# Inverting the softmax sums inside the attention stages, and splitting later weights on GpSimd in the first one

## The chip, the cores and the metric

The kernel runs on one core of a Trainium2 chip. The metric is the device time of one execution in microseconds (us), as the median of several runs. The program is one chain of stages on one core: every engine takes part in every stage, and a barrier of all engines stands between two stages.

## The reference

Two cross-attention layers run one after the other. x is 4096 x 512, the context 3202 x 512, all in float32. The first layer has 8 heads of 16, the second 16 heads of 32.

```
q, k, v  = projections of x (or of its layernorm) and of the context
attn     = softmax(q k^T / sqrt(hd));   o = attn v
layer 1:   X = x + o W_o;      x1  = relu(X w1^T + b1) w2^T + b2 + X
layer 2:   q from layernorm(x1);  X = x1 + o Wo^T + bo;  out = X + silu(X W1^T + b1) W2^T + b2
```

The attention kernels store the unnormalised `exp(...) v` (`acc`) and the row sums (`sums`); the stage behind divides. Products of float32 matrices are built from three TensorE products of halves: a matrix is split into `hi` (rounded to the TensorE's float32r) and `lo` (what is left), and `hi hi + hi lo + lo hi` is accumulated.

## The kernel before

The stages are `front` (keys, values, first queries), `attention` "a0" (layer 1), `middle` "m" (the rest of layer 1, layernorm, second queries), `attention` "a1" (layer 2) and `ending` "e".

**Attention.** An *item* is one head and one block of 512 queries: 64 items in a0, 128 in a1. A head's keys fill 26 tiles of 128. For an item TensorE computes 26 score tiles (L535), ScalarE the exponentials (L441), TensorE the weighted sums of v in batches (L561). For the items ahead, TensorE computes scores a second time in 28 *units* (L526) and VectorE reduces each from PSUM (L465), which gives the row maximum; SP moves it through DRAM into the query tile (`move_row`, L336 and L340). In a0 the sums of the exponentials come from a column of ones in v. In a1 GpSimd adds up most exponential tiles in nine steps per item (L407 to L421), VectorE adds six others (L482), and a last matmul with ones (L556) finishes the sum. ScalarE copies the accumulator out (L428), SP stores it (L346 to L353).

SP issues all transfers of a stage in the order of its program: per item the query tile of the next item (`a_q`, L331), the query tile of the maxima of the item after that (`a_qm`, L331), the store of the item before, `move_row`, and at each head's first item the keys and values of the head after it (`load_kv`, L320 and L324). TensorE's first unit that reads a newly loaded `a_qm` stands at tile 14 of the 26 of an item.

**Weights.** In a0 VectorE splits Wo of layer 2 in the last item (`split_weights`, L488 and L490), and SP stores the halves to DRAM. In a1 the four row blocks of W1 are loaded whole at the start (L362) and split by VectorE in the last item ahead of its work of that item; the halves stay in SBUF for the ending. The middle stage loads W_o, w1, w2 and splits them itself on ScalarE and VectorE (L1647, L1724).

**Start of the middle and of the ending.** SP loads all sums as 128 rows (`total`), VectorE inverts them (L1802, L1448), SP stores them to DRAM (`recips`) and loads them back, each head's row spread over the partitions of that head (L1597, L1297). Only then can the first block be normalised (L1731, L1415) and split, which TensorE's first product (L1857, L1484) waits for. In the middle TensorE then computes the query bias (L1907) from Wq, which is the last transfer that SP issues there, and only after it the first hidden layer.

Of the kernel before, what the change touches and what calls it, by code (L numbers as in the profile page):

```python
# [26 lines left out]
P = 128  # L27
# [157 lines left out]
def attention(nc, name, H, hd, q, k, v, row, acc_out, sums_out, weights=(), keep=()):  # L185
# [17 lines left out]
    with phase(nc, name) as (ctx, sb, ps, sem):  # L203
# [5 lines left out]
        prob = sb("prob", [P, ST, NB], F32)  # L209
        acc_sb = [sb(f"acc_sb{i}", [P, NB], F32) for i in range(2)]  # L210
# [21 lines left out]
        ones_made = sem("ones_made")  # L232
        add_done, acc_copied, vsum_done = sem("add_done"), sem("acc_copied"), sem("vsum_done")
# [3 lines left out]

        w_loaded, w_hi, w_lo, w_kept = sem("w_loaded"), sem("w_hi"), sem("w_lo"), sem("w_kept")

# [5 lines left out]
        SPLIT_AT = 0  # L245
# [59 lines left out]

        q_items = q.rearrange("h b s r c -> (h b) s r c")
# [3 lines left out]
        def _(sp):  # L310
# [30 lines left out]

            def store(h, qb, j, n):
                sp.wait_ge(acc_copied, n + 1)
                cols = bass.ds(qb * NB, NB)
                for i in range(ATEND):
                    sp.dma_start(acc_out[i, bass.ds(h * hd, hd), cols],  # L346
                                 acc_sb[j][i * 32:i * 32 + hd, :]).then_inc(acc_stored[j], 16)
                if APART:
                    sp.wait_ge(side_copied, n + 1)
                    sp.dma_start(acc_out[ATEND, bass.ds(h * hd, hd), cols], side[3 * 32:P, :]).then_inc(side_stored, 16)  # L350
                for i in range(SUMS):
                    at = 3 * 32 if APART else i * 32 + hd
                    sp.dma_start(sums_out[i, bass.ds(h, 1), cols],  # L353
                                 acc_sb[j][at:at + 1, :]).then_inc(acc_stored[j], 16)
# [38 lines left out]
            sp.wait_ge(w_kept, 16 * len(keep))  # L393

        @block.gpsimd
        def _(pool):
            fill(pool, 1)

# [61 lines left out]
        def _(dve):  # L460
# [24 lines left out]
            def split_weights():  # L485
                dve.wait_ge(w_loaded, 16 * len(weights))
                for i, (_, whole, hi, lo) in enumerate(weights):
                    dve.tensor_copy(hi, whole).then_inc(w_hi, 1)  # L488
                    dve.wait_ge(w_hi, i + 1)
                    dve.tensor_tensor(lo, whole, f32(hi), ALU.subtract).then_inc(w_lo, 1)  # L490
# [11 lines left out]
            for it in items(dve):  # L502
                for t in range(ST):
                    if it.last and weights and t == SPLIT_AT:

                        split_weights()
# [7 lines left out]
            if weights:  # L514
                dve.wait_ge(w_lo, len(weights))
# [702 lines left out]
def ending(nc, name, acc, sums, recips, x, wo_split, bo, W1, b1, func, w2, b2, out):  # L1218
# [22 lines left out]
    spread = [t.rearrange("h (c t) -> (h c) t", c=P // H) for t in (sums[0], recips)]  # L1241

    with phase(nc, name) as (ctx, sb, ps, sem):
# [8 lines left out]

        total = h[1]
        assert H * T // P == NB
# [32 lines left out]
        def _(sp):  # L1287
# [12 lines left out]
            def next_acc(n, k):  # L1300

                sp.wait_ge(ol_done, n * KT + k)
                load_acc(n, k)
                load_recips(n, k)
# [28 lines left out]
            load_wo(0, 3)  # L1333
            for m in range(FT):
# [72 lines left out]
        def _(dve):  # L1407
# [39 lines left out]
            dve.wait_ge(sums_loaded, 16)  # L1447
            dve.reciprocal(total[:], total[:]).then_inc(recip_done, 1)  # L1448
            for k in range(KT):
                normalise(0, k)  # L1450
                split_o(0, k)
            for d in range(KT):
                add_x(0, d)
# [70 lines left out]
def middle(nc, name, acc, sums, recips, x, wo, w1, b1, w2, b2, gamma, beta, wq, x1, q):  # L1524
# [13 lines left out]
    spread = [t.rearrange("h (c t) -> (h c) t", c=P // H) for t in [sums[i] for i in range(SIDE)] + [recips]]  # L1538

    with phase(nc, name) as (ctx, sb, ps, sem):  # L1540
# [5 lines left out]
        total = sb("total", [P, SIDE, H * T // P], F32)  # L1546
# [18 lines left out]
        staged = {"wo": (std[:].unsqueeze(1), WO), "w1": (y[:], W1), "w2": (early[0], W2)}  # L1565
# [20 lines left out]
        W_ORDER = ["wo", "w1", "w2", "wq"]  # L1586
# [3 lines left out]
        def _(sp):  # L1590
# [14 lines left out]

            for i in range(SIDE):
                sp.dma_start(total[:, i], spread[i]).then_inc(sums_loaded, 16)
            load_weight("wo", staged["wo"][0], wo)
            load_acc(0)
            load_weight("w1", staged["w1"][0], w1)  # L1610
            for to, dram in ((bias1[:], b1), (bias2[:], b2), (gb[:, 0, :], gamma), (gb[:, 1, :], beta)):
                sp.dma_start(to, dram[:, :]).then_inc(const_loaded, 16)
            sp.wait_ge(recip_done, 1)
            sp.dma_start(spread[SIDE], total[:, 0]).then_inc(recips_stored, 16)
            load_xin(0)
            sp.wait_ge(recips_stored, 16)
            load_recips(0)
            load_weight("w2", staged["w2"][0], w2)
            load_weight("wq", sq[:], wq)
            for n in range(-1, BLOCKS + 1):  # L1620
                if 0 <= n + 2 < BLOCKS:

                    sp.wait_ge(ol_done, n + 2)
                    load_acc(n + 2)
                    load_recips(n + 2)
# [17 lines left out]
        def _(act):  # L1643
            def split_weight(n):
                stage, (hi, _) = staged[n]
                act.wait_ge(w_loaded[n], 16)
                act.activation(hi[:], stage, ACT.Copy).then_inc(w_hi, 1)  # L1647

# [40 lines left out]
            split_weight("wo")  # L1689
            split_weight("w1")  # L1690
            split_o(0)
            split_weight("w2")
# [7 lines left out]
            act.wait_ge(w_lo, len(W_ORDER))  # L1700
# [19 lines left out]
        def _(dve):  # L1720
            def split_weight(i, n):
                stage, (hi, lo) = staged[n]
                dve.wait_ge(w_hi, i + 1)
                dve.tensor_tensor(lo[:], stage, f32(hi[:]), ALU.subtract).then_inc(w_lo, 1)  # L1724

# [71 lines left out]
            dve.memset(inv_d[:], 1.0 / D).then_inc(consts_done, 1)  # L1797
            dve.wait_ge(sums_loaded, 16 * SIDE)
# [4 lines left out]
            split_weight(0, "wo")  # L1803
            split_weight(1, "w1")
            normalise(0)
            split_o(0)
            split_weight(2, "w2")
            add_x(0)
            split_x(0)
# [4 lines left out]
            dve.wait_ge(w_hi, 4)  # L1814
# [36 lines left out]
        def _(pe):  # L1851
# [16 lines left out]
            def hidden(n):  # L1868
                pe.wait_ge(xl_done, n + 1)
                if n == 0:  # L1870
                    pe.wait_ge(w_lo, 2)
# [5 lines left out]
            def project(n, tiles):  # L1877
                if n == 0:
                    pe.wait_ge(w_lo, 3)
# [7 lines left out]
            def queries(n):  # L1887
                pe.wait_ge(ycl_done, n + 1)
                if n == 0:
                    pe.wait_ge(w_lo, 4)  # L1890
# [10 lines left out]
            pe.wait_ge(w_lo, 1)  # L1901
# [35 lines left out]
def build(nc, a, out):  # L1937
# [20 lines left out]
    wo_split = scratch("wo_split", [KT, 2, P, KT, P])  # L1958
    with ExitStack() as ctx:
        WO = weight(nc, ctx, "wo", KT, D)  # L1960
        whole = ctx.enter_context(nc.sbuf_tensor("wo_whole", [P, KT, D], F32))
        attention(nc, "a0", *L0, q[0], k[0], v[0], row, acc[0], sums[0],
                  [(a["L1_xattn_Wo"].rearrange("(k p) c -> p k c", p=P), whole[:], WO[0][:], WO[1][:])],
                  [(wo_split[d, i], WO[i][:, :, d * P:(d + 1) * P]) for d in range(KT) for i in range(2)])
    middle(nc, "m", acc[0], sums[0], recips[0], x, a["L0_xattn_W_o"], a["L0_xattn_w1"], a["L0_xattn_b1"],
           a["L0_xattn_w2"], a["L0_xattn_b2"], a["L1_xattn_ln_q_g"], a["L1_xattn_ln_q_b"], a["L1_xattn_Wq"], x1, q[1])
    with ExitStack() as outer:
        W1 = weight(nc, outer, "w1", KT, a["L1_xattn_W1"].shape[1])
        with ExitStack() as inner:
            whole = inner.enter_context(nc.sbuf_tensor("w1_whole", [P, KT, a["L1_xattn_W1"].shape[1]], F32))  # L1970
            attention(nc, "a1", *L1, q[1], k[1], v[1], row, acc[1], sums[1],
                      [(src, whole[:, i, :], W1[0][:, i, :], W1[1][:, i, :])
                       for i, src in enumerate(rows(a["L1_xattn_W1"], a["L1_xattn_W1"].shape[1]))])
# [30 lines left out]
```

## Time and profile before

| what | value |
| --- | --- |
| median of 3 runs | 5425.91 us (5416.05 to 5426.97) |
| the profiled execution, its own time | 5431.3 us |
| its span | 5429.5 us |
| PE busy | 5216.4 us (96%) |
| VectorE (DVE) busy | 4277.0 us (79%) |
| ScalarE (ACT) busy | 3251.5 us (60%) |
| GpSimd (POOL) busy | 2485.7 us (46%) |
| DMA | 341.18 MB, 63 GB/s over the span |

The stages can be told apart by the tile names (`kv_`, `a_`, `m_`, `e_`). a0 and a1 both use `a_`; a0 ends and the middle begins at 1444 us, the middle's products end at 1819 us, a1 lasts until 4557 us, and the ending fills the rest. "SPq" rows are DMA issues of SP. The granted clock of TensorE (PEclk) is given as a share: 1.00 is 2.4 GHz, 0.50 is 1.2 GHz.

### The profile page before, as it was taken

How to read it: one execution, taken by the hardware profiler on the slowest of the kernel's cores; microseconds unless marked ns; L12 is line 12 of the kernel's file. 1: busy time of each engine (PE TensorE's matmuls, PEld its weight loads, DVE VectorE, ACT ScalarE, POOL GpSimd, SP SyncE). 2: the span in 40 equal slices, each digit the busy share in tenths (PEclk: the TensorE clock that was granted, in tenths of full speed). 3: DMA queues.
4: the chain of work that ended last, by engine and by line, in shares of the span. 5: the costliest groups of instructions: out<-in, count | busy, mean ns of one | idle time of the engine just before them, and what ended most of it. 6: DMA issues, size and time to landing. Idle time of an engine off the chain costs nothing. (4 is left out here: it accounts for less than half of the span.)

```text
span 5429.5 us, 93007 instructions
## 1 busy us (share of the span) xinstructions
PE 5216.4 (96%) x27916; PEld 3335.3 (61%) x27916; DVE 4277.0 (79%) x6970; ACT 3251.5 (60%) x5920; POOL 2485.7 (46%) x1165
## 2 busy tenths in 40 slices
PE   8989999999799799999999999999999995999999
PEld 6844444444377566666666666666666662788887
DVE  6689999999577799999999999999999995432331
ACT  4258888888533377777777777777777773322222
POOL 0000000000000299999999999999999995000000
PEclk9989999999799799999999999999999997999999
DMA  7521111111344311111111111111111112332320
GB/s 218 130 51 36 38 39 39 38 37 32 93 124 128 107 33 45 46 45 46 37 41 45 46 45 45 32 46 45 46 45 33 45 33 86 117 97 87 100 93 24
DMA packets 340342, 341.18 MB, mean 63 GB/s; under 512 B 188304, under 2 KB 196368, under 8 KB 337936
## 3 DMA queue, kind: packets, MB, share of 16 engines
q1 hardware_dynamic: 339984, 336.71, 23.5%
q8 instruction: 188, 3.08, 0.2%
q14 instruction: 170, 1.39, 0.1%
HBM read 227.57 MB, written 108.92 MB: 62 GB/s over the span
## 5 line engine op out<-in xcount | busy, mean ns | idle before, releaser
L465 DVE TENSOR_REDUCE a_maxes<-a_mscore 128x1 f32<-128x458 f32 (+4 forms) x5376 | 3044.8, 626 | 218.6 <-PE a_mscore L526 163.1
L441 ACT ACTIVATE a_prob<-a_score 128x512 f32<-128x512 f32 x4992 | 2635.6, 602 | 891.8 <-PE a_score L535 855.9
L535 PE MATMUL a_score<-a_q,a_k 97*128 97x512 f32 (+1 forms) x4992 | 1937.1, 434 | 23.6 <-ACT a_prob L441 8.0
L526 PE MATMUL a_mscore<-a_k,a_qm 96*128 96x458 f32 (+4 forms) x5376 | 1837.8, 412 | 36.1 <-DMA a_k<-k 33.9
L410 POOL TENSOR_TENSOR a_added<-a_added,a_prob 128x1024 f32<-128x1024 f32 x640 | 1533.7, 2396 | 71.0
L526 PEld LDWEIGHTS a_mscore<-a_k,a_qm 96*128 96x128 f32 (+1 forms) x5376 | 1456.4, 309 | 131.2 <-DVE a_maxes L465 49.8
L535 PEld LDWEIGHTS a_score<-a_q,a_k 97*128 97x128 f32 (+1 forms) x4992 | 916.1, 193 | 974.4 <-ACT a_prob L441 587.1
L561 PE MATMUL a_acc<-a_prob,a_v 128*32 128x512 f32 x9984 | 1469.1, 604 | 1.1 <-ACT a_prob L441 0.7
L304 POOL MEMSET a_k<- 32x126 f32 (+4 forms) x6 | 6.3, 1053 | 1821.9 <-POOLq L60 1821.6
L556 PE MATMUL a_acc<-a_prob,a_ones 128*1 128x512 f32 x1280 | 611.6, 592 | 0.0
L482 DVE TENSOR_REDUCE a_vsum<-a_prob 128x256 f32<-128x768 f32 x512 | 528.5, 1033 | 31.6 <-POOL a_added L416 30.3
L1438 DVE TENSOR_TENSOR e_hl<-e_h,e_hh 128x512 fp32r<-128x512 f32 x128 | 88.6, 692 | 533.0 <-ACT e_hh L1387 533.0
L561 PEld LDWEIGHTS a_acc<-a_prob,a_v 128*32 128x32 f32 x9984 | 276.6, 109 | 322.5 <-issue 205.9
L1383 ACT ACTIVATE e_h<-e_hp,e_bias 128x512 f32<-128x512 f32 x128 | 88.3, 690 | 562.5 <-PE e_hp L1495 562.5
L407 POOL TENSOR_TENSOR a_added<-a_prob 128x1024 f32<-128x1024 f32 x128 | 305.9, 2389 | 134.6 <-ACT a_prob L441 134.4
L416 POOL TENSOR_TENSOR a_added<-a_added,a_vsum 128x1024 f32<-128x1024 f32 x128 | 305.6, 2387 | 14.5 <-POOL a_added L413 0.4
L428 ACT ACTIVATE a_acc_sb<-a_acc 97x512 f32<-97x512 f32 (+1 forms) x192 | 114.7, 598 | 181.8 <-PE a_acc L556 176.2
L1495 PE MATMUL e_hp<-e_xh,w_hi 128*128 128x512 f32 x512 | 204.0, 398 | 7.6 <-DVE e_xl L1430 7.6
L1495 PE MATMUL e_hp<-e_xl,w_hi 128*128 128x512 f32 x512 | 203.0, 397 | 0.0
L1495 PE MATMUL e_hp<-e_xh,w_lo 128*128 128x512 f32 x512 | 203.0, 397 | 0.0
L413 POOL TENSOR_TENSOR a_added<-a_added,a_prob 128x512 f32<-128x512 f32 x128 | 166.9, 1304 | 14.5 <-ACT a_prob L441 0.4
L421 POOL TENSOR_TENSOR a_total<-a_added 128x512 f32<-128x512 f32 x128 | 166.1, 1298 | 10.0
(208 smaller groups left out, 4063.3 us busy)
## 6 DMA issues: line engine op xcount, KB each, us to landing
e_part<-acc SPq DMA_DIRECT2D x120, 256.0 KB, 3.8
a_qm<-q SPq DMA_DIRECT2D x384, 64.0 KB, 1.9
a_q<-q SPq DMA_DIRECT2D x384, 64.0 KB, 1.9
acc<-a_acc_sb SPq DMA_DIRECT2D x384, 64.0 KB
a_k<-k SPq DMA_DIRECT2D x48, 416.0 KB, 6.6
q<-m_qout SPq DMA_DIRECT2D x128, 128.0 KB, 2.3
e_wo<-wo_split SPq DMA_DIRECT2D x32, 512.0 KB, 4.9
k<-kv_k1out SPq DMA_DIRECT2D x24, 512.0 KB, 2.9
```

Of the source, the lines that this page charges most:

```text
L407: pool.tensor_tensor(added[:], prob[:, 0:2], prob[:, 10:12], ALU.add).then_inc(add_done, 1)
L410: pool.tensor_tensor(added[:], added[:], prob[:, t:t + 2], ALU.add).then_inc(add_done, 1)
L413: pool.tensor_tensor(added[:, 0], added[:, 0], prob[:, 22], ALU.add).then_inc(add_done, 1)
L416: pool.tensor_tensor(added[:], added[:], vsum[:], ALU.add).then_inc(add_done, 1)
L441: act.activation(prob[:, t], score[SCORES[it.j][t]][:], ACT.Exp, scale=SCALE).then_inc(exp_done, 1)
L465: dve.tensor_reduce(maxes[j][:, t, c:c + 1], mscore[u % UNIT_BANKS][:, 0:wide], AX.X, ALU.max).then_inc(unit_read, 1)
L482: dve.tensor_reduce(vsum[:, which, cols], prob[:, tiles[0]:tiles[-1] + 1, cols].rearrange("p t c -> p c t"), AX.X, ALU.add).then_inc(vsum_ ...
L526: pe.matmul(mscore[u % UNIT_BANKS][:, 0:wide], qm[j][r:r + ROW, t:NB:NB // P], kt[kk][r:r + ROW, at:at + wide], start=True, stop=True).the ...
L535: pe.matmul(score[SCORES[it.j][t]][:], kt[it.k][r:r + C, i * P:(i + 1) * P], qt[it.j][r:r + C, :], start=True, stop=True).then_inc(score_d ...
L556: mm = pe.matmul(acc[c * 32:c * 32 + 1, :], ones[:, col:col + 1], total[:] if what[0] == "sum" else prob[:, what[1]], start=start, stop=stop)
L561: mm = pe.matmul(acc[c * 32:c * 32 + 32, :], vt[kk][:, L.FIRST[half] + at, :], prob[:, what], start=start, stop=stop)
L1495: mm = pe.matmul(hp[m % 2][:], W1[a][:, k, m * P:(m + 1) * P], (xh, xl)[c][:, k], start=(t == 0), stop=(t == 3 * KT - 1))
```

## The change

Both attentions, in the last item, load the sums of all items but the last, add them up and invert them on VectorE, and store the reciprocals. The middle and the ending begin with `acc` and these reciprocals; they load the last item's sums as 128 x 4 numbers, invert those, and store them before the last block.

In a0 GpSimd splits W_o, w1, w2 of layer 1, Wo and the four row blocks of W1 of layer 2: eight jobs through one whole tile and two half tiles. SP runs them from `later_weights`, at each head's first item (ahead of `load_kv`) and at its sixth: it stores the halves of one job to DRAM and loads the next weight. The middle loads halves instead of whole weights; a1 loads the halves of W1, one of the eight at each such step. VectorE's `split_weights` goes.

```diff
 attention, SP:
-            for dram, whole, _, _ in weights:
-                sp.dma_start(whole, dram).then_inc(w_loaded, 16)
+            def later_weights(step):
+                if 0 <= step - 2 < len(splits):
+                    job = splits[step - 2]
+                    sp.wait_ge(w_lo, step - 1)
+                    for i, half in enumerate(halves):
+                        for c, to in enumerate(job[3]):
+                            wide = job[2] // len(job[3])
+                            sp.dma_start(to[i], f32(piece(half, job)[:, :, c * wide:(c + 1) * wide])).then_inc(w_kept, 16)
+                if 0 <= step - 1 < len(splits):
+                    job = splits[step - 1]
+                    if step > 1:
+                        sp.wait_ge(w_lo, step - 1)
+                    sp.dma_start(piece(whole, job), job[0]).then_inc(w_loaded, 16)
+                if 0 <= step - 1 < len(loads):
+                    to, dram = loads[step - 1]
+                    sp.dma_start(f32(to), dram).then_inc(w_loaded, 16)
...
+                if it.starts_head or (isinstance(it.qb, int) and it.qb == QB - 3):
+                    later_weights(it.h * 2 + (0 if it.starts_head else 1))
                 if it.starts_head and not it.first and not it.final_head:
                     load_kv(it.h + 1, 1 - it.k)
                 if it.last:
-                    for to, half in keep:
-                        sp.wait_ge(w_lo, len(weights))
-                        sp.dma_start(to, f32(half)).then_inc(w_kept, 16)
+                    sp.wait_ge(acc_stored[1 - it.j], H * (QB // 2) * STORED)
+                    sp.wait_ge(acc_stored[it.j], (H * (QB // 2) - 1) * STORED)
+                    for i in range(SUMS):
+                        sp.dma_start(sums_all[0:BUT_LAST, i], spread[i][0:BUT_LAST]).then_inc(sums_loaded, 16)
+                    sp.wait_ge(recip_done, 1)
+                    sp.dma_start(spread[SUMS][0:BUT_LAST], sums_all[0:BUT_LAST, 0]).then_inc(recips_stored, 16)
                     store(it.h, it.qb, it.j, it.n)
 attention, GpSimd:
+            for i, job in enumerate(splits):
+                pool.wait_ge(w_loaded, 16 * i + 16)
+                if i:
+                    pool.wait_ge(w_kept, KEPT[i])
+                hi, lo = (piece(half, job) for half in halves)
+                pool.tensor_copy(hi, piece(whole, job)).then_inc(w_hi, 1)
+                pool.wait_ge(w_hi, i + 1)
+                pool.tensor_tensor(lo, piece(whole, job), f32(hi), ALU.subtract).then_inc(w_lo, 1)
 attention, VectorE (split_weights goes; at tile 20 of the last item):
+            def invert():
+                dve.wait_ge(sums_loaded, 16 * SUMS)
+                for i in range(1, SUMS):
+                    dve.tensor_tensor(sums_all[0:BUT_LAST, 0], sums_all[0:BUT_LAST, 0], sums_all[0:BUT_LAST, i],
+                                      ALU.add).then_inc(summed, 1)
+                    dve.wait_ge(summed, i)
+                dve.reciprocal(sums_all[0:BUT_LAST, 0], sums_all[0:BUT_LAST, 0]).then_inc(recip_done, 1)
 ending, SP (VectorE inverts the last item's total behind the four first splits):
-            sp.dma_start(total[:], spread[0]).then_inc(sums_loaded, 16)
             load_acc(0, 0)
+            load_recips(0, 0)
             load_acc(0, 1)
+            load_recips(0, 1)
             for to, dram in ((biaso[:], bo), (bias1[:], b1), (bias2[:], b2)):
...
-            sp.wait_ge(recip_done, 1)
-            sp.dma_start(spread[1], total[:]).then_inc(recips_stored, 16)
-            sp.wait_ge(recips_stored, 16)
-            load_recips(0, 0)
-            load_recips(0, 1)
+            sp.dma_start(total[:], spread[0]).then_inc(sums_loaded, 16)
 middle, SP (split_weight goes on ScalarE and VectorE):
+            load_acc(0)
+            load_recips(0)
+            load_halves("wo", WO)
+            load_xin(0)
+            load_halves("w1", W1)
+            for to, dram in ((bias1[:], b1), (bias2[:], b2), (gb[:, 0, :], gamma), (gb[:, 1, :], beta)):
+                sp.dma_start(to, dram[:, :]).then_inc(const_loaded, 16)
+            load_halves("w2", W2)
             for i in range(SIDE):
                 sp.dma_start(total[:, i], spread[i]).then_inc(sums_loaded, 16)
...
             load_weight("wq", sq[:], wq)
```

## Rows read from the trace of the kernel before

**Rows 1.** Windows of a0 and a1: stretch, length, each engine's busy time, PEclk, DMA, GB/s

```profile
500.00:1380.00 880.00, 873.35 (x5352) 433.43 (x5348) 807.26 (x1467) 715.37 (x1364) 0.00 (x0) 1.00 0.17 37
2000.00:4490.00 2490.00, 2478.28 (x14065) 1545.54 (x14065) 2343.42 (x3933) 1770.02 (x3338) 2297.87 (x1073) 1.00 0.17 42
```

**Rows 2.** Timeline of POOL near a1's end: start, length, line, out<-in, count, idle before

```profile
4459.68 2.39 POOL L407 TENSOR_TENSOR a_added<-a_prob 128x1024 f32<-128x1024 f32 x1 [1.03 <-ACT a_prob L441]
...
4478.32 1.28 POOL L421 TENSOR_TENSOR a_total<-a_added 128x512 f32<-128x512 f32 x1
...
4501.28 2.38 POOL L407 TENSOR_TENSOR a_added<-a_prob 128x1024 f32<-128x1024 f32 x1 [0.47 <-ACT a_prob L441]
...
4526.36 3.19 POOL L421 TENSOR_TENSOR a_total<-a_added 128x512 f32<-128x512 f32 x1
...
4551.24 1.26 POOL L421 TENSOR_TENSOR a_total<-a_added 128x512 f32<-128x512 f32 x1
```

**Rows 3.** Line 490, VectorE's subtractions: ns min/median/max, first and last start

```profile
L490 DVE TENSOR_TENSOR w_lo<-w_whole,w_hi x4: 4309/4336/4357, 4509.8 to 4530.7; 128x2048 fp32r<-128x2048 f32 x4
```

**Rows 4.** Timeline of ACT near a1's end

```profile
4531.51 0.60 ACT L428 ACTIVATE a_acc_sb<-a_acc 97x512 f32<-97x512 f32 x1 [8.43 <-PE a_acc L556]
```

**Rows 5.** Timelines of SP, DVE and PE at the start of the ending

```profile
4559.27 0.36 SPq L1315 DMA_DIRECT2D e_h<-sums  x1
...
4569.88 3.35 DVE L1448 RECIPROCAL e_h<-e_h 128x512 f32<-128x512 f32 x1 [31.08 <-DMA e_bias<-in_L_xattn_b]
4579.29 2.14 DVE L1413 TENSOR_TENSOR e_part<-e_part 128x512 f32<-128x512 f32 x3 [6.06 <-DMA e_part<-recips]
...
4600.02 0.79 PE L1484 MATMUL e_ap<-e_oh,e_wo 128*128 128x512 f32 x1 [45.60 <-DVE e_ol L1419]
```

**Rows 6.** Timelines of SP, DVE and PE at the start of the middle

```profile
1444.19 1.78 SPq L1607 DMA_DIRECT2D m_total<-sums  x4
...
1456.59 3.57 SPq L1597 DMA_DIRECT2D m_part<-recips  x8
...
1461.76 2.15 DVE L1729 TENSOR_TENSOR m_part<-m_part 128x512 f32<-128x512 f32 x3 [1.80 <-DMA m_part<-recips]
...
1471.41 3.73 PE L1907 MATMUL m_var<-m_gb,m_sq 128*128 128x1 f32 x32
1475.55 0.77 PE L1857 MATMUL m_prod<-m_xh,m_w_hi 128*128 128x512 f32 x1 [0.41 <-issue]
```

**Rows 7.** Windows with busy DMA: the last two numbers are DMA share and GB/s

```profile
465.40:473.40 8.00, 7.93 (x46) 4.59 (x47) 7.60 (x15) 6.07 (x12) 0.00 (x0) 1.00 0.94 122
1846.00:1854.00 8.00, 8.00 (x16) 4.54 (x15) 7.96 (x16) 0.00 (x0) 0.00 (x0) 0.50 1.01 422
5336.00:5337.00 1.00, 1.00 (x7) 0.79 (x6) 0.69 (x1) 0.23 (x1) 0.00 (x0) 1.00 1.07 418
1446.00:1458.00 12.00, 0.00 (x0) 0.00 (x0) 3.90 (x6) 2.54 (x2) 0.00 (x0) 0.50 0.98 327
```

**Rows 8.** Timeline of SP in a0 at the first item of head 2

```profile
591.49 2.63 SPq L331 DMA_DIRECT2D a_q<-q  x6
...
604.28 2.62 SPq L320 DMA_DIRECT2D a_k<-k  x6
...
609.06 3.75 SPq L331 DMA_DIRECT2D a_q<-q  x6
613.01 2.67 SPq L331 DMA_DIRECT2D a_qm<-q  x6
```

**Rows 9.** Waits of PE in a0: waited for, us in total, times, longest

```profile
PE a_mscore L526 <- DMA a_qm<-q: 0.2, 1, 0.2
```

**Rows 10.** Timelines of SP and PE at a1's start

```profile
1852.68 0.33 SPq L336 DMA_DIRECT2D row<-a_negmax  x1
1856.38 0.24 SPq L340 DMA_DIRECT2D a_q<-row  x1
...
1857.95 0.76 PE L535 MATMUL a_score<-a_q,a_k 97*128 97x512 f32 x1 [1.23 <-DMA a_q<-row]
```

More of the change, by code:

```diff
@@ L182, with attention @@
 VSUMS = len(ON_VECTOR) * PIECES
-def attention(nc, name, H, hd, q, k, v, row, acc_out, sums_out, weights=(), keep=()):
+def attention(nc, name, H, hd, q, k, v, row, acc_out, sums_out, recips, splits=(), loads=()):
     SCALE = float(hd) ** -0.5
@@ L232, in attention @@
         ones_made = sem("ones_made")
+        sums_loaded, summed, recip_done, recips_stored = (
+            sem("sums_loaded"), sem("summed"), sem("recip_done"), sem("recips_stored"))
         add_done, acc_copied, vsum_done = sem("add_done"), sem("acc_copied"), sem("vsum_done")
@@ L235, in attention, with piece @@
         acc_stored = [sem(f"acc_stored{i}") for i in range(2)]
+        if splits:
+            whole = sb("whole", [P, KT * D], F32)
+            halves = [sb(f"half{i}", [P, KT * D], F32R) for i in range(2)]
         w_loaded, w_hi, w_lo, w_kept = sem("w_loaded"), sem("w_hi"), sem("w_lo"), sem("w_kept")
+        KEPT = [16 * sum(2 * len(job[3]) for job in splits[:i]) for i in range(len(splits) + 1)]
+        def piece(tile, job):
+            return tile[:, 0:job[1] * job[2]].rearrange("p (k c) -> p k c", k=job[1])
         LOADS = 16 * 3 * HALVES
@@ L243, in attention @@
         STORED = 16 * (ATEND + SUMS)
-        SPLIT_AT = 0
+        RECIP_AT = 20
         def items(eng):
@@ L304, in fill @@
                 eng.memset(ap, value).then_inc(filled[i], 1)
+        spread = [t.rearrange("h (c t) -> (h c) t", c=P // H) for t in [sums_out[i] for i in range(SUMS)] + [recips]]
+        BUT_LAST = P - P // (H * QB)
         q_items = q.rearrange("h b s r c -> (h b) s r c")
@@ L392, in _ @@
                 sp.wait_ge(side_stored, 16 * H * QB)
-            sp.wait_ge(w_kept, 16 * len(keep))
+            sp.wait_ge(w_kept, KEPT[-1])
+            sp.wait_ge(w_loaded, 16 * (len(splits) + len(loads)))
+            sp.wait_ge(recips_stored, 16)
         @block.gpsimd
@@ L483, in add_up @@
                                   AX.X, ALU.add).then_inc(vsum_done, 1)
[L485 to L490, printed above, removed]
+            def invert():
[5 more added lines that the diff above has]
+                dve.reciprocal(sums_all[0:BUT_LAST, 0], sums_all[0:BUT_LAST, 0]).then_inc(recip_done, 1)
             fill(dve, 0)
@@ L503, in _ @@
                 for t in range(ST):
-                    if it.last and weights and t == SPLIT_AT:
-                        split_weights()
                     for ahead, u in units_of(it, t):
@@ L513, in _ @@
                         add_up(it.n, it.first, *divmod(L.sum_at.index(t), PIECES))
-            if weights:
-                dve.wait_ge(w_lo, len(weights))
+                    if it.last and t == RECIP_AT:
+                        invert()
         @block.tensor
@@ L1239, in ending @@
     A_AT, ADD_AT = (11, 12, 13, 14), (12, 13, 14, 15)
-    spread = [t.rearrange("h (c t) -> (h c) t", c=P // H) for t in (sums[0], recips)]
+    spread = [t[H - 1, T - NB:T].rearrange("(p t) -> p t", p=P) for t in (sums[0], recips)]
     with phase(nc, name) as (ctx, sb, ps, sem):
@@ L1300, in next_acc @@
             def next_acc(n, k):
+                if n == BLOCKS - 1 and k == 0:
+                    sp.wait_ge(recips_stored, 16)
                 sp.wait_ge(ol_done, n * KT + k)
@@ L1333, in _ @@
             load_wo(0, 3)
+            sp.wait_ge(recip_done, 1)
+            sp.dma_start(spread[1], total[:]).then_inc(recips_stored, 16)
             for m in range(FT):
@@ L1451, in _ @@
                 split_o(0, k)
+            dve.wait_ge(sums_loaded, 16)
+            dve.reciprocal(total[:], total[:]).then_inc(recip_done, 1)
             for d in range(KT):
@@ L1521, in _, with middle @@
                 use_hidden(n, FT - 1)
-def middle(nc, name, acc, sums, recips, x, wo, w1, b1, w2, b2, gamma, beta, wq, x1, q):
+def middle(nc, name, acc, sums, recips, x, split, b1, b2, gamma, beta, wq, x1, q):
     H, BLOCKS, HT = sums.shape[1], T // NB, KT
@@ L1536, in middle @@
     HEADS = P // QD
-    spread = [t.rearrange("h (c t) -> (h c) t", c=P // H) for t in [sums[i] for i in range(SIDE)] + [recips]]
+    spread = [t[H - 1, T - NB:T].rearrange("(p t) -> p t", p=P) for t in [sums[i] for i in range(SIDE)] + [recips]]
     with phase(nc, name) as (ctx, sb, ps, sem):
@@ L1604, in load_weight, with load_halves @@
                 sp.dma_start(to, dram.rearrange("(k p) c -> p k c", p=P)).then_inc(w_loaded[n], 16)
+            def load_halves(n, to):
+                for half, dram in zip(to, split[n]):
+                    sp.dma_start(f32(half[:]), dram).then_inc(w_loaded[n], 16)
+            load_acc(0)
[6 more added lines that the diff above has]
+            load_halves("w2", W2)
             for i in range(SIDE):
                 sp.dma_start(total[:, i], spread[i]).then_inc(sums_loaded, 16)
[L1608 to L1618, printed above, removed]
             load_weight("wq", sq[:], wq)
@@ L1624, in _ @@
                     load_acc(n + 2)
+                    if n + 2 == BLOCKS - 1:
+                        sp.wait_ge(recip_done, 1)
+                        sp.dma_start(spread[SIDE], total[:, 0]).then_inc(recips_stored, 16)
+                        sp.wait_ge(recips_stored, 16)
                     load_recips(n + 2)
@@ L1720, in _ @@
         def _(dve):
[L1721 to L1724, printed above, removed]
             def normalise(n):
@@ L1797, in _ @@
             dve.memset(inv_d[:], 1.0 / D).then_inc(consts_done, 1)
+            normalise(0)
+            split_o(0)
+            add_x(0)
+            split_x(0)
             dve.wait_ge(sums_loaded, 16 * SIDE)
@@ L1958, in build @@
     wo_split = scratch("wo_split", [KT, 2, P, KT, P])
-    with ExitStack() as ctx:
[L1960 to L1973, printed above, removed]
+    F = a["L1_xattn_W1"].shape[1]
@@ new lines, in build, with tiles @@
+    first = {n: scratch(f"first_{n}", [2, P, kt, D]) for n, kt in (("wo", 1), ("w1", KT), ("w2", KT))}
+    w1_split = scratch("w1_later", [KT, 2, P, 1, F])
+    def tiles(w):
+        return w.rearrange("(k p) c -> p k c", p=P)
+    splits = [(tiles(a[f"L0_xattn_{n}"]), kt, D, [[first[m][i] for i in range(2)]])
+              for n, m, kt in (("W_o", "wo", 1), ("w1", "w1", KT), ("w2", "w2", KT))]
+    splits.append((tiles(a["L1_xattn_Wo"]), KT, D, [[wo_split[d, i] for i in range(2)] for d in range(KT)]))
@@ new lines, in build @@
+    splits += [(tiles(a["L1_xattn_W1"][r * P:(r + 1) * P, :]), 1, F, [[w1_split[r, i] for i in range(2)]])
+               for r in range(KT)]
+    attention(nc, "a0", *L0, q[0], k[0], v[0], row, acc[0], sums[0], recips[0], splits)
+    middle(nc, "m", acc[0], sums[0], recips[0], x, first, a["L0_xattn_b1"], a["L0_xattn_b2"], a["L1_xattn_ln_q_g"],
+           a["L1_xattn_ln_q_b"], a["L1_xattn_Wq"], x1, q[1])
+    with ExitStack() as ctx:
+        W1 = weight(nc, ctx, "w1", KT, F)
+        attention(nc, "a1", *L1, q[1], k[1], v[1], row, acc[1], sums[1], recips[1],
+                  loads=[(W1[i][:, r:r + 1, :], w1_split[r, i]) for r in range(KT) for i in range(2)])
```

36 lines of the change are left out of this document (9 added, 27 removed).

## The prediction

> **What bounds the kernel now.** I read the windows first. In the long attention stretches TensorE is busy 873.35 of 880 us in a0 and 2478.28 of 2490 us in a1, at full clock [rows 1]: whatever stalls TensorE there is lost, and work of other engines there is free as long as nobody waits for it. In a1 GpSimd is nearly as full (2297.87 us). So the seams matter: the timelines at the end of a1 and at the starts of the two stages behind the attentions, where TensorE waits, and then SP's queue in a0, where the change puts new transfers. The times below are those of the profiled execution (5431.3 us, span 5429.5); the median of the runs is 5.4 us lower, and I subtract the sum from the median. A difference under about 0.2% (11 us) can't be told from no change here.
>
> **End of a1: removed splits.** GpSimd's chain of an item runs from its first add to `a_total`: undisturbed 4459.68 to 4478.32 + 1.28, so 19.92 us. In the last item but one it takes 4501.28 to 4529.55, 28.27 us, and the last one ends at 4552.50, 22.95 us later [rows 2]. Beside both lie VectorE's four splits, of which the subtractions alone take 4.34 us each, the last from 4530.7 on [rows 3]. The accumulator copy waits 8.43 us for the late sum [rows 4]. Without the splits the first chain ends at 4501.28 + 19.92 = 4521.2. The last item's chain then needs its 12th exponential: ScalarE's four exponentials of tiles 10 to 13 ended at 4531.51 - 8.43 = 4523.08, the 12th a microsecond earlier, so it starts at 4522.1 and ends at 4542.0. That is 10.5 us earlier; TensorE, ScalarE and the stores behind it move along.
>
> The added inversion lies beside it: SP stores the item before (copy at about 4525, five issues), loads the sums, VectorE inverts for at most 3.35 us [rows 5], and SP stores the result around 4537, before SP is needed for the last store near 4544. What is queued behind SP's new waits is only that last store. Nothing shows a reciprocal beside GpSimd; from both sides it costs 0 to 3.35 x (28.27/19.92 - 1) = 1.4 us. I take 0, since it is one short instruction.
>
> **Start of the ending.** Before: first issue 4559.27, VectorE waits until 4569.88 for the constants (issued behind nine large loads), inverts, SP stores and reloads, and the first sum starts at 4579.29, 20.0 us after the first issue; TensorE starts at 4600.02, 20.7 us after that [rows 5]. After: SP issues 8 `acc` and 8 reciprocal loads at 0.45 us each (3.57 us for eight [rows 6]) and three constants, about 8.7 us. In front of the constants lie 2.62 MB instead of 2.36; at the pace before (10.6 us for those) they land near 12 us, and the first sum can start. That is 8 us earlier; the four chunks behind it keep their 20.7 us, since SP's second pair waits for VectorE as before. The bounds: 9.4 us if the constants land as early as before, 5.5 us if they land 2.5 us later than I think. I take 7.5. The last item's inversion and its store are small and behind the four splits.
>
> **Start of the middle.** Before, the first normalisation starts at 1461.76, 17.6 us after the first issue, and the first hidden layer at 1475.55, 31.4 us [rows 6]. After, twelve issues take 5.4 us, normalisation can start near 7 us, and the 13.8 us from there to the hidden layer would put that near 21 us. What is late next is Wq: TensorE does the bias product (3.73 us [rows 6]) before the hidden layer, Wq is SP's last load, and the halves double the bytes in front of it: 0.52 + 1.05 + 2.10 + 2.10 + 1.05 = 6.8 MB after the first 6 us. At 422 GB/s for the 4.7 MB of halves and 327 for the rest [rows 7] it lands near 25 us; the bias product then starts behind an idle TensorE and takes 4 to 5 us. The hidden layer starts near 30 us: a gain of 1.5 us out of the 10.6 that the removed path promises. At 327 GB/s for all of it the gain is -0.6; without the clock's share it is 2.5. The removed splits on ScalarE and VectorE were in that path and are worth nothing more.
>
> **Start of a1.** The four W1 loads go. Before, the first row store was issued while 4 MB were moving at 422 GB/s [rows 7]; its load could follow only 3.70 us later and TensorE waited 1.23 us [rows 10]. I take 1, between 0 and 1.2. The halves come one 1 MB load per half head; SP has one more issue there: 0.
>
> **a0: new traffic.** GpSimd has a job of two 2048-wide operations; the subtraction is twice a 2.39 us add [rows 2], 4.8 us, the copy is 0 to 4.8, so under 10 us of the three items or more (52 us) that lie between load and store. VectorE's slowdown is bounded by 8 x 9.6 x 0.42 = 32 us, against 73 us of idle time in the stretch [rows 1]: I take 0. The removed Wo split lies in the last item, off the path: 0.
>
> The transfers are another matter. One queue serves SP's DMAs, and rows 10 show that a later small one waits for the bytes ahead. At the first item of heads 2, 3 and 4 SP now issues, ahead of `load_kv`, two 1.05 MB stores and a 1.05 MB load. Count from the old first `a_k` issue, 604.28: first bytes at 0.8 us, stores 2.10 MB at 418 GB/s 5.0, load 2.5 at 422, then keys and values, which keep the engines 8.0 x 0.94 = 7.5 us [rows 7]: the queue is empty at 15.8, and the twelve `a_q` and `a_qm` loads behind it land at about 17.7 (1.2 of transfer, 0.7 to land). TensorE needs `a_qm` at tile 14 of 26: the item starts with SP's `a_q` issue at 609.06, one item is 17.57 us, so at 4.8 + 9.4 = 14.2 [rows 8]. Before, `a_qm` landed about 1 us ahead of that, and TensorE waited for it once, 0.2 us [rows 9]: there is no slack. Three stalls of 3.5 us make 10.6, and I take 11. Head 1 has half the store (0.52 MB) and just passes; the sixth items have no keys behind them, and their 3 MB are through about 3.5 us into the next item: 0. The ends: 0 if the engines serve the small loads beside the large ones; 31 if SP's issue itself is held until the queue is empty (twelve issues of 0.45 and 1.7 to land after 15.8 make 22.9, 8.7 us late three times, and 4.9 once at head 1).
>
> Weights and halves may also move more slowly: the middle's first loads ran at 327 GB/s [rows 7]. At that rate the 3.15 MB take 9.6 us instead of 7.5, three stalls are 6.4 us longer, and the middle's gain is -0.6: the sum is 8.5 us worse. The Trainium skill's "DMA: Bandwidth & Descriptors", section Specifications, puts a core's limit at the HBM near 358 GB/s, between that and the 422 and 418 that rows 7 show for such transfers; by the page the sum would be about 5 us worse, an estimate from its figure. The measured rates are above it, so the sum goes by them.
>
> **Sum.** 10.5 + 7.5 + 1.5 + 1 - 11 = 9.5 us less: 5425.9 - 9.5 = 5416.4 us.
>
> **Rivals.**
> - *The queue costs nothing in a0.* For it: engines may take small transfers past large ones on other rings. Against: rows 10. Time: 5425.9 - 20.5 = 5405.4.
> - *Issue is held, slower.* Place: SP at the first items of heads 1 to 4. If SP can't issue the query loads until values and halves have drained, the price is 31 us: 5425.9 + 31 - 20.5 = 5436.4. It turns slower from the point where the stalls exceed 20.5 us in sum. For it: `a_q` behind the values takes 3.75 us instead of 2.63 [rows 8]. Against: that is 1.1 us, not the whole drain.
> - *The new transfers run at 327 GB/s,* as the middle's first loads did, with 2 KB rows; against it, the 422 GB/s of whole weight rows: 5425.
> - *The change doesn't hide the inversion:* SP waits for the reciprocal ahead of the last store; were it 7 us later than I count, the end of a1 would lose up to 5 of its 10.5 us: 5421.
>
> **How the numbers follow.** Forecast 0.42 (its own range 5409 to 5424); no queue cost 0.28; issue held 0.16; slower transfers 0.08; inversion not hidden 0.06. Faster by over 0.2% (under 5415.1): 0.17 of the forecast's 0.42 and 0.27 of the first rival, 0.44. Slower by over 0.2% (above 5436.8): half of the held issue and a little of the others, 0.11. The rest, 0.45, lies within. The range takes in the first rival and most of the way to the second: 5403 to 5432.
>
> **What would show it.** End of a1: GpSimd's last two chains at 20 us each, and no wait of 8 us before the accumulator copy. Ending: TensorE's first product some 33 us after the first issue instead of 40.8. Middle: TensorE waiting for Wq before the bias product, the hidden layer near 30 us. a0: TensorE waits of 3 to 4 us for `a_qm` at heads 2, 3 and 4, and none elsewhere. The forecast is wrong if these waits are absent, if they stand at every step, or if the last store of a1 waits for SP.

## The result and the profile after

The changed kernel takes 5450.13 us (median of 5 runs, 5444.38 to 5454.63), the kernel before 5416.45 us in runs beside it (5 runs, 5414.63 to 5426.97): the ratio is 1.0057, 95% interval 1.0045 to 1.0068. It is slower by 24 to 37 us; the forecast was 5416.4, within 5403 to 5432.

The profiled execution after took 5452.02 us (span 5450.2), 20.7 us of span more than the one of before. Cut at the same events, the two spans compare like this (us; the first stretch begins with the span, each other one where the line above ends):

| stretch, up to | before | after | difference |
| --- | --- | --- | --- |
| SP's last row load in a0 | 1404.30 | 1442.39 | +38.1 |
| the middle's first issue | 39.89 | 28.93 | -11.0 |
| the first hidden layer's first product | 31.36 | 34.48 | +3.1 |
| the end of a1's last `a_total` | 3076.95 | 3065.34 | -11.6 |
| the ending's first issue | 6.77 | 15.38 | +8.6 |
| TensorE's first product of the ending | 40.75 | 33.51 | -7.2 |
| the end of the span | 829.48 | 830.17 | +0.7 |

**a0.** The waits of TensorE after (waited for, us in total, times, longest), where before it was 0.2 us, once [rows 9]:

```profile
PE a_mscore L571 <- DMA a_qm<-q: 29.2, 5, 8.0
```

SP's queue at head 2 after (start, length, line, transfer, count), the answer to [rows 8]:

```profile
610.94 0.82 SPq L365 DMA_DIRECT2D first_w<-a_half  x2
611.80 0.91 SPq L370 DMA_DIRECT2D a_whole<-in_L_xattn_Wo  x1
612.75 5.19 SPq L335 DMA_DIRECT2D a_k<-k  x6
617.98 0.55 SPq L339 DMA_DIRECT2D a_v<-v  x1
618.91 8.92 SPq L346 DMA_DIRECT2D a_q<-q  x6
628.03 2.66 SPq L346 DMA_DIRECT2D a_qm<-q  x6
```

TensorE there and at head 1 (in brackets the wait before the instruction and what ended it):

```profile
484.15 0.92 PE L571 MATMUL a_mscore<-a_k,a_qm 48*128 48x418 f32 x2 [5.07 <-DMA a_qm<-q]
...
632.18 0.92 PE L571 MATMUL a_mscore<-a_k,a_qm 48*128 48x418 f32 x2 [6.82 <-DMA a_qm<-q]
```

And the windows around head 2's wait (stretch, length, TensorE's busy time, granted clock, DMA share, GB/s):

```profile
622.00:624.00 2.00, 2.00 (x19) 1.00 0.99 139
624.00:626.00 2.00, 1.36 (x10) 1.00 1.66 89
626.00:628.00 2.00, 0.00 (x0) 0.95 0.33 74
...
636.00:638.00 2.00, 2.00 (x12) 0.50 0.07 9
638.00:640.00 2.00, 1.93 (x13) 0.99 0.00 1
```

Read the three together. The six `a_q` issues take 8.92 us where they took 3.75, and end as the DMA engines' share falls off; `a_qm` is issued behind them, so it is SP's issue that is late, not the transfer. The issue of the keys is stretched as well, 5.19 us instead of 2.62 [rows 8], behind the stores and the load alone. Heads 3 and 4 show the same with waits of 7.74 and 7.97 us. The fifth wait, 1.58 us, follows the transfers at head 2's sixth item, where a job goes out in eight stores. TensorE resumes at half clock (0.50, 1.2 GHz) and is back at full only near 638, so this stall costs more than its wait; over the five, the stretch is 38.1 us longer for 29.2 us of waits.

**The last item of a0** is where the two spans come closer than the medians. In the profile of before TensorE's clock falls to 0.50 in that item; after it doesn't. The windows of before (stretch, length, TensorE's busy time, granted clock, DMA share, GB/s):

```profile
1400.00:1410.00 10.00, 9.21 (x55) 1.00 0.05 8
1410.00:1420.00 10.00, 9.53 (x30) 0.50 0.06 14
```

and those of after:

```profile
1440.00:1450.00 10.00, 9.01 (x52) 1.00 0.01 1
1450.00:1460.00 10.00, 9.51 (x58) 1.00 0.23 65
```

The tail behind the last row load is 39.89 us or 28.9 accordingly. That is 11 us which the profiled execution of before lost there, and no gain of the change: a variant of the changed kernel lost them too (last experiment).

**The middle** after, SP and then TensorE, the answer to [rows 6]:

```profile
1483.88 4.18 SPq L1663 DMA_DIRECT2D m_total<-sums  x4
1488.11 0.63 SPq L1648 DMA_DIRECT2D m_sq<-in_L_xattn_Wq  x1
```

```profile
1498.95 6.99 PE L1940 MATMUL m_var<-m_gb,m_sq 128*128 128x1 f32 x32 [10.65 <-DMA m_sq<-in_L_xattn_Wq]
1505.80 0.77 PE L1890 MATMUL m_prod<-m_xh,m_w_hi 128*128 128x512 f32 x1
```

TensorE stands 10.65 us for Wq, then needs 6.99 us for the bias product that took 3.73 [rows 6]; the granted clock is 0.50 all through it.

**The end of a1**: GpSimd's last two chains after, the answer to [rows 2]:

```profile
4528.85 2.38 POOL L454 TENSOR_TENSOR a_added<-a_prob 128x1024 f32<-128x1024 f32 x1 [0.49 <-ACT a_prob L488]
...
4550.94 2.40 POOL L454 TENSOR_TENSOR a_added<-a_prob 128x1024 f32<-128x1024 f32 x1 [1.86 <-ACT a_prob L488]
...
4569.88 1.26 POOL L468 TENSOR_TENSOR a_total<-a_added 128x512 f32<-128x512 f32 x1
```

Both take 20.2 us; the two together are 42.3 us from 4528.85 to 4571.14, where before they were 51.2 [rows 2]. But the inversion beside them is late. SP, VectorE and the windows while the sums' load runs:

```profile
4556.54 0.24 SPq L421 DMA_DIRECT2D a_sums_all<-sums  x1
4571.96 0.22 SPq L423 DMA_DIRECT2D recips<-a_sums_all  x1
...
4586.52 1.78 SPq L1335 DMA_DIRECT2D e_part<-acc  x4
```

```profile
4568.58 3.35 DVE L538 RECIPROCAL a_sums_all<-a_sums_all 127x512 f32<-127x512 f32 x1 [16.87 <-DMA a_sums_all<-sums]
```

```profile
4561.00:4565.00 4.00, 1.00 0.07 26
...
4580.00:4584.00 4.00, 0.50 0.07 26
```

(In the windows: stretch, length, granted clock, DMA share, GB/s.)

127 rows of 2 KB take 12 us at 26 GB/s, with a DMA share of 0.07: about one of the 16 engines works. The load of 128 such rows in the kernel before (KB, us from issue to landing):

```profile
e_h<-sums SPq DMA_DIRECT2D x1, 256.0 KB, 2.6
```

The store of the reciprocals after goes the same way until near 4586, and the ending waits for it. The last store of the accumulator does not: SP has issued the reciprocals at 4571.96 and issues it at 4573.72, 2.6 us behind the end of the last `a_total`.

**The ending** after, the answer to [rows 5]: from its first issue at 4586.52 to the first sum 12.8 us instead of 20.0.

```profile
4599.29 2.14 DVE L1458 TENSOR_TENSOR e_part<-e_part 128x512 f32<-128x512 f32 x3 [27.36 <-DMA e_bias<-in_L_xattn_b]
```

### The profile page after: what moved, and what is told of

Read it like the earlier page. It is cut to its first block and busy times, and to the rows that moved or that the text cites. A ratio compares the mean times of both kernels' runs of the same rounds, so it can differ in the third digit from the quotient of the medians.

```text
span 5450.2 us, 93056 instructions
## 1 busy us (share of the span) xinstructions
PE 5217.1 (96%) x27916; PEld 3335.2 (61%) x27916; DVE 4241.8 (78%) x6962; ACT 3247.7 (60%) x5917; POOL 2520.8 (46%) x1181
## 5 line engine op out<-in xcount | busy, mean ns | idle before, releaser
L442 POOL CAST a_half<-a_whole 128x2048 fp32r<-128x2048 f32 (+1 forms) x8 | 13.9, 1732 | 598.9 <-DMA a_whole<-in_L_xattn_W 275.3
```

## Experiments

A *burst* is what one call of `later_weights` issues in a0: the stores of one job's halves and the load of the next weight, 3.15 MB at heads 2, 3 and 4. All runs but the last start from the changed kernel. Ratios are to the kernel before in the same set of runs, differences to the changed kernel are between medians of different sets; the kernel before had 5416.45 us in the set of the result, 5418.16 with the moved bursts, the keys and values, the rows and Wq, and 5421.22 with the other four. The intervals of keys and values first, of the rows and of Wq overlap with that of the changed kernel (1.0045 to 1.0068), so for these three it is the traces that show the gain.

**The bursts of a0 in other items.**

```diff
-                if it.starts_head or (isinstance(it.qb, int) and it.qb == QB - 3):
-                    later_weights(it.h * 2 + (0 if it.starts_head else 1))
+                if isinstance(it.qb, int) and it.qb in (QB - 3, QB - 1):
+                    later_weights(it.h * 2 + (it.qb == QB - 1))
```

> Only the place of the bursts in a0 (and of the single loads in a1) is changed: they go to the sixth and the eighth item of each head, away from the head's first item, in which the next head's keys and values are loaded. Theory A (the values, in 64-byte pieces, lie behind the burst in the queue, and SP's issue of the next queries is held until they have drained): TensorE's waits for a_qm in a0 fall from 29.2 us to under 4, the issue of the six a_q loads is back to about 3 us everywhere, and the time falls by 27 us to about 5423. Rival B (the bytes of a burst delay the queries of whatever item follows it, about 1.6 us as after the eight-store burst of head 2): five to eight waits stay, 8 to 13 us in sum, about 5431 to 5436. Rival C (the lost time in a0 is GpSimd's splitting beside VectorE): no waits for a_qm, but a0 hardly shorter, 5445 to 5450.

5417.13 us (12 runs): 33 us less than the changed kernel, and level with the kernel before (0.9998, 0.9987 to 1.0009). TensorE's waits:

```profile
PE a_mscore L571 <- DMA a_qm<-q: 1.7, 1, 1.7
```

SP at a head's first item without the burst, then at a sixth item with a burst of the same size:

```profile
611.45 3.52 SPq L346 DMA_DIRECT2D a_q<-q  x6
...
694.50 0.82 SPq L365 DMA_DIRECT2D first_w<-a_half  x2
...
698.35 3.58 SPq L346 DMA_DIRECT2D a_q<-q  x6
```

Theory A held for the place and the waits; the time fell by 33 instead of 27, which fits the clock behind each stall. The one wait of 1.7 us follows the burst with eight stores. Rival C falls as well: GpSimd still does all eight splits, and a0's last row load is issued at 1410.19, 32.2 us earlier than in the changed kernel. From its first row load to its last, a0 takes 1097.6 us before, 1135.8 in the changed kernel and 1101.1 here: of 38.2 us, 34.7 go with the bursts, and 3.5 stay, 1.7 of them the wait.

**Keys and values ahead of the burst.** The two blocks of the same item change places, `load_kv` first, then `later_weights`.

> In a0 the same burst stays in the head's first item, but keys and values are issued ahead of it instead of behind it; the bytes in front of the next queries are the same 3.8 MB. Theory A (values behind the burst hold the issue): the values drain at once, the six a_q loads are issued in 3 to 4 us instead of 9, and only the bytes are left to delay a_qm, by the forecast's own count 3.5 us at heads 2, 3 and 4 and about 1 at head 1: TensorE waits 11 us for a_qm instead of 29, about 5432. Rival B (any 3 MB that lie ahead delay the queries alike, whatever their order): 29 us of waits and a_q issues of 9 us stay, 5450.

5439.94 us (1.0041, 1.0027 to 1.0055): 10 us less, where A said 18 and B none.

```profile
PE a_mscore L571 <- DMA a_qm<-q: 20.4, 5, 5.8
```

```profile
609.73 0.56 SPq L339 DMA_DIRECT2D a_v<-v  x1
610.33 3.55 SPq L365 DMA_DIRECT2D first_w<-a_half  x2
...
615.23 4.62 SPq L346 DMA_DIRECT2D a_q<-q  x6
```

Whatever stands right behind the values is held: here the stores take 3.55 us for two instead of 0.82, and `a_q` 4.62 instead of 8.92. So the hold is real, but the order alone returns only 8.8 of the 29.2 us; in what is left, the bytes and the hold that remains are not told apart.

**The values in another item.** The burst stays in the head's first item, ahead of the keys; `load_v` moves.

```diff
+                if isinstance(it.qb, int) and it.qb == QB - 2 and 0 < it.h < H - 1:
+                    load_v(it.h + 1, 1 - it.k)
```

> The bursts stay in a0 where the change put them, in the head's first item ahead of the next head's keys; only the load of the values, in 64-byte pieces, is moved out of that item, to the head's seventh. Theory A (it is the values' slow pieces behind the burst that hold the issue and keep the engines at 1 to 1.7 of share with 100 GB/s): the six a_q loads are issued in about 3 us, and what is left is 3.15 MB and the keys, as in the sixth item of head 2 (1.58 us of wait): TensorE waits for a_qm under 6 us in all instead of 29.2, about 5426. Rival B (3 MB of bytes ahead of the queries are enough): 15 us of waits and more stay, 5436 or above.

5433.8 us (12 runs; 1.0030, 1.0019 to 1.0040), between the two theories.

```profile
PE a_mscore L577 <- DMA a_qm<-q: 12.5, 4, 4.0
```

The transfers of the stretch 600 to 622 us (count, KB each, median us from issue to landing), and the same two of the changed kernel in 608 to 634:

```profile
a_q<-q SPq DMA_DIRECT2D x6, 32.0 KB, 7.4
a_qm<-q SPq DMA_DIRECT2D x6, 32.0 KB, 5.9
```

```profile
a_q<-q SPq DMA_DIRECT2D x6, 32.0 KB, 1.8
a_qm<-q SPq DMA_DIRECT2D x6, 32.0 KB, 1.7
```

SP in that stretch:

```profile
603.06 5.11 SPq L335 DMA_DIRECT2D a_k<-k  x6
608.55 2.68 SPq L350 DMA_DIRECT2D a_q<-q  x6
```

The transfers and SP's issues tell the two mechanisms apart. Without the values SP issues `a_q` in 2.68 us and the loads lie 7.4 and 5.9 us in a full queue: the mechanism of the forecast, with waits of 4.04, 2.69 and 3.88 us at heads 2, 3 and 4 and none at head 1. With the values SP is held until they have drained, and each load then lands in 1.8 us. So 12.5 us of the waits stay with burst and keys, and 16.7 us go with the values. The values are not all that holds SP: the keys' issue, right behind the burst, takes 5.11 us here too. Whether SP is held by the number of pieces that wait, by their bytes or by their slow rate, no run separates. The values' pieces are 64 bytes: 3889 of 5013 packets in that stretch of the changed kernel are under 512 B, 551 of 1681 without the values. The Trainium skill's "DMA: Bandwidth & Descriptors", section Specifications, gives 512 B as the least piece for full rate; the trace agrees, with 139 and 89 GB/s at shares of 0.99 and 1.66 in the windows of the changed kernel at 622 and 624 us.

**127 rows as 112 and 15.**

```diff
+        PARTS = [slice(0, 112), slice(112, BUT_LAST)]
-                        sp.dma_start(sums_all[0:BUT_LAST, i], spread[i][0:BUT_LAST]).then_inc(sums_loaded, 16)
+                        for part in PARTS:
+                            sp.dma_start(sums_all[part, i], spread[i][part]).then_inc(sums_loaded, 16)
```

(and the same for the store)

> The load of the sums and the store of the reciprocals by 127 partitions (126 in a0) are each cut into one of 112 and one of 15 (14). Theory A (a transfer of 127 partitions is moved by one of the 16 DMA engines: 25 GB/s and a DMA share of 0.06 while it runs): the load lands about 3 us after its issue instead of 12, the store likewise, SP stands ready before the last accumulator copy, and from the last a_total to the ending's first issue it is about 7 us instead of 15.4: the time falls by 8.5 us to about 5441.5. Rival B (the load waits for the late stores of the sums or for GpSimd's and VectorE's traffic, and the number of partitions is no matter): landing stays near 12 us, 5450. In a0, where the inversion was hidden, both expect no change.

5443.11 us (1.0043, 1.0028 to 1.0057), 7.0 less than the changed kernel. SP and VectorE:

```profile
4557.19 0.80 SPq L423 DMA_DIRECT2D a_sums_all<-sums  x2
4563.32 0.79 SPq L426 DMA_DIRECT2D recips<-a_sums_all  x2
4572.96 1.27 SPq L380 DMA_DIRECT2D acc<-a_acc_sb  x3
...
4577.19 1.79 SPq L1338 DMA_DIRECT2D e_part<-acc  x4
```

```profile
4559.94 3.35 DVE L541 RECIPROCAL a_sums_all<-a_sums_all 127x512 f32<-127x512 f32 x1 [8.29 <-DMA a_sums_all<-sums]
```

The reciprocal starts 2.75 us after the first issue instead of 12.04, SP stands ready 9 us before the last store, and from the last `a_total` (end 4570.38) to the ending it is 6.81 us instead of 15.38, by 8.6 us the whole loss of that seam. Theory A holds for the 127 rows. The Trainium skill's "DMA: Bandwidth & Descriptors", section "Why a DMA increments its semaphore by 16 and not by 1", says why: a transfer uses the largest number of engines up to 16 that divides the outer size of both its sides, here the partitions, and 127 partitions are named as running on one. The trace of the changed kernel agrees (share 0.07, 26 GB/s).

Theory A's "(126 in a0)" is wrong: in the changed kernel a0's four loads by 126 partitions move at 256 GB/s together, at a share of 0.82 (a window as above):

```profile
1458.00:1459.00 1.00, 1.00 (x11) 1.00 0.82 256
```

**Wq ahead of w1's and w2's halves** (W1 and W2 in the expectations).

```diff
             load_xin(0)
-            load_halves("w1", W1)
+            load_weight("wq", sq[:], wq)
             for to, dram in ((bias1[:], b1), (bias2[:], b2), (gb[:, 0, :], gamma), (gb[:, 1, :], beta)):
                 sp.dma_start(to, dram[:, :]).then_inc(const_loaded, 16)
+            load_halves("w1", W1)
             load_halves("w2", W2)
...
-            load_weight("wq", sq[:], wq)
```

> In the middle the load of Wq (1.05 MB) and the constants are issued ahead of the halves of W1 and W2 instead of behind them and the sums. Theory A (TensorE's bias product waits for Wq, the last of 7.5 MB): Wq lands some 13 us after the stage's first issue instead of 27.6, the bias product runs before xl is ready, and the hidden layer starts 22 to 25 us after the first issue instead of 34.5: 10 to 12 us less, about 5439. Rival B (W1's halves, now behind Wq, are what TensorE waits for in its place): hidden layer at 28 to 30, 5 us less, about 5445. Rival C (the sums' small loads and the reciprocal, not Wq, set the path): no gain, 5450.

5444.48 us (1.0051, 1.0037 to 1.0065), 5.7 less. From the first issue at 1468.50 to the hidden layer it is 27.0 us instead of 34.5:

```profile
1488.80 6.83 PE L1940 MATMUL m_var<-m_gb,m_sq 128*128 128x1 f32 x32 [3.48 <-DMA m_gb<-in_L_xattn_ln_q_b]
```

Wq was the wait, but A's 22 to 25 was missed: a small constant behind Wq ends the wait now, and the product still runs 6.83 us, most of it at a granted clock of 0.50. B's 5445 fits the time, but not its reason: w1's halves are not waited for.

**The three edits together.** (first, fourth and fifth of the above)

> The three edits together: bursts at the sixth and eighth item, 127 rows as 112 and 15, Wq ahead of W1's and W2's halves. Theory A (three separate causes, one behind the other on TensorE's path): their gains over the changed kernel add up, 33.0 + 7.0 + 5.7 us by the medians of the single runs, 5404 us, which is under the kernel before by 0.2 to 0.3%. Rival B (part of what one saves is lost again at the next stage, whose loads start earlier against the same stores): 5410 to 5415, no difference to the kernel before that can be told.

5403.05 us, ratio to the kernel before 0.9963 (0.9950 to 0.9977): faster by 0.23 to 0.50%, and as expected by A. By the ratios of the single runs, each to the kernel before in its own set, the sum would have been 0.9978, just above that interval; each ratio is only known to 0.0011 to 0.0014, so the times don't show that the gains add up exactly. The trace shows all three in place: the ending starts 6.81 us after the last `a_total`, the middle's hidden layer 23.2 us after its first issue, and one `a_qm` wait is left:

```profile
PE a_mscore L574 <- DMA a_qm<-q: 2.4, 1, 2.4
```

**The constants first as well.** The loop over `bias1` to `beta` moves ahead of `load_xin`.

> As the three edits together, but the middle's four small constants are issued ahead of the inputs and of Wq. Theory A (with Wq early, TensorE's bias product waited 3.48 us for the small constant behind it, m_gb): the product starts as W_o's product ends, some 16 us after the first issue instead of 20.3, and the hidden layer at 22 to 24 us instead of 27: 3 to 5 us less than the three edits alone. Rival B (the product runs for 6.8 us at the lower clock in any case and Wq itself lands near 20 us): hidden layer at 26 to 27, no gain.

5403.61 us (0.9966, 0.9954 to 0.9978): no gain, as B had it, though not for B's reason. The bias product starts earlier, and TensorE waits 1.69 us for a half of w1 in its place; the hidden layer starts 22.3 us after the first issue against 23.2. A's place for the hidden layer (22 to 24) is met and its gain is not, since with the three edits the wait for the constant had already shrunk from 3.48 to 1.26 us:

```profile
1457.60 3.88 PE L1943 MATMUL m_var<-m_gb,m_sq 128*128 128x1 f32 x32
1463.16 0.77 PE L1893 MATMUL m_prod<-m_xh,m_w_hi 128*128 128x512 f32 x1 [1.69 <-DMA m_w_lo<-first_w]
```

**The kernel before, profiled again.**

> The kernel before, unchanged, for a second profile: the medians of before and after lie 33.7 us apart, their two profiled spans 20.7. If the first profile of before was one of its longer executions, this one shows a span near 5412 to 5416 and the stage in which the 13 us lie; if it is the profiler that adds them, the span is near 5429 again.

5424.7 us, span 5422.9: between the two expectations. Its clock falls in a0's last item too, and the tail behind the last row load is again 39.89 us (first row below to the second):

```profile
1401.58 0.52 SPq L340 DMA_DIRECT2D a_q<-row  x2
1441.47 0.84 SPq L1607 DMA_DIRECT2D m_total<-sums  x2
```

The experiment with moved bursts shows it as well (39.93), the other seven profiles don't (28.9). The runs of the kernel before beside the last four lie between 5412.27 and 5431.25, at mean granted clocks from 0.979 down to 0.975, which fits this tail being half speed in some of them; only profiled executions show it directly.

## Why the prediction was wrong, step by step

- **a0, the failed step: "Three stalls of 3.5 us make 10.6, and I take 11."** There were five, 29.2 us in all, and with the clock behind each the stretch lost 38.1. The rival "Issue is held, slower", given 0.16, is what happened: its price of 31 us stands against 27.6 us of waits at heads 1 to 4 (5.07, 6.82, 7.74, 7.97), and its 5436.4 is too low mainly for want of the clock, the late inversion and the middle (below). I had argued against it that the held `a_q` issue of [rows 8] cost "1.1 us, not the whole drain". But in those rows only keys and values had to drain, with nothing large ahead of them: the row was the mechanism at its smallest, and I read it as its size. That head 1 "just passes" fell with it (5.07 us); the sixth items' 0 held but for the eight-store burst (1.58).
- **The mechanism that I had counted exists too.** With the values away, heads 2, 3 and 4 wait 4.04, 2.69 and 3.88 us. Their 10.6 us in sum are the forecast's figure, but by luck: I had reached it with the values included in the bytes, a sum too short by their time.
- **No price for the clock.** I charged a stall at its wait. After head 2's wait TensorE runs at 0.50 until about 638, and the stretch with the five waits lost 8.9 us beyond their sum. Up to 1.8 of these may be something else, since that much stays beyond the one wait when the bursts are moved.
- **"The added inversion lies beside it" failed**: I priced VectorE's 3.35 us and, in effect, took the load for one like the 128-row load of before; the landing of the store I did not price at all. One row fewer made 12 us of the load, and the store as much: 8.6 us. My rival for this had up to 5, at another place: SP was ready for the last store in time, and it is the end of the stage that waited for the reciprocals to land.
- **The middle, +1.5 forecast, -3.1 found.** The order of the argument was right (normalisation starts 7.2 us after the first issue, then all waits for Wq). Wq landed at 27.6 us instead of 25, behind the sums' small loads (4.18 us of issue), and the bias product took 6.99 us, all at 0.50, instead of 4 to 5.
- **Right**: the ending (7.5 forecast, 7.2 found); a1's chains at 20 us each (10.5 forecast, 8.9 between the first add and the last total; the accumulator copy of the last item but one waits 1.01 us instead of 8.43 [rows 4]); the start of a1 (row store to its load 2.30 us instead of 3.70 [rows 10], 1.4 for a forecast of 1); no cost of VectorE's reciprocal to GpSimd's chain beside it (20.18 us where the 127 rows were cut in two and it ran in the middle of the chain); GpSimd's splits cost at most the 1.8 us above.

In the sum, gains of 20.5 us were forecast. 18.8 came, 11.6 up to the last total of a1 and 7.2 in the ending; against them stand 38.1 of a0, 8.6 of the inversion, 3.1 of the middle and 0.7 behind it all. By the two profiles the kernel loses 20.7 us, of which the tail in before's profile hides 11; without it the difference is 31.7, near the 33.7 of the medians.

## What to carry to other kernels

Large background transfers are best issued where nothing with a deadline follows at once, and above all not ahead of a load in small pieces: here the issue of what stood right behind that load was held. Count a hidden transfer's partitions before calling it hidden: 127 rows took 12 us where 128 took 2.6, and cut into 112 and 15 they landed within 2.75. A stall of TensorE can be dearer than its wait, because the clock returns late.

## What the hardware showed unexpectedly

A DMA of 127 partitions moved 254 KB at 26 GB/s, while four of 126 ran at 256 GB/s together; cut in two, the 127 landed within 2.75 us. An issue of six 32 KB loads took 8.92 us behind 64-byte pieces that queued behind 3 MB, 3.58 us behind the same 3 MB alone. TensorE's clock fell to 0.50 in the last item of a0 in three of the ten profiles, with a busy share of 0.90 to 0.92 in the 10 us around it, and stayed at full in the other seven with 0.90; what decides it is open.
